# Column maxima of a softmax by VectorE block transposes, and seven VectorE instructions moved, in a fused cross-attention kernel

## The reference

```
proj    = memory @ W_mem.T                       # 1601 x 512
scores  = x @ proj.T / sqrt(512)
attn    = softmax(scores, axis=-1)               # over the 1601 memory rows
ctx     = attn @ proj
gate    = sigmoid(concat(x, ctx) @ W_gate.T + b_gate)
fused   = x + gate * ctx
out     = fused * rsqrt(mean(fused**2) + eps) * norm_w
```

## Time and profile before

| what | us |
|---|---|
| median of 3 runs | 545.79 (545.26 to 546.56) |
| the profiled execution's own time | 546.02 |
| its span | 544.0 |
| PE busy | 533.3 (98% of the span) |
| DVE busy | 480.4 (88%) |
| ACT busy | 315.9 (58%) |
| POOL busy | 148.0 (27%) |
| granted TensorE clock | 0.998 |

### The profile page before, as it was taken

The page is one execution under the profiler, slowest core; times in us unless marked ns, Lnnn a source line. Parts: engine busy times, 40 slices in busy tenths (PEclk is TensorE's granted clock), DMA queues, the critical chain, the costliest instruction groups (busy, mean ns, idle before and its releaser), DMA issues.

```text
span 544.0 us, 8854 instructions
## 1 busy us (share of the span) xinstructions
PE 533.3 (98%) x2420; PEld 436.6 (80%) x2420; DVE 480.4 (88%) x758; ACT 315.9 (58%) x601; POOL 148.0 (27%) x127
## 2 busy tenths in 40 slices
PE   8899999999999999999999999999999999999994
PEld 7776888888888888888888888888888888888883
DVE  3779958899799997999978998989979999789967
ACT  4575636566465664666465763656556575557523
POOL 0005610065002540036200660015400263004703
PEclk9999999999999999999999999999999999999999
DMA  9855363621576207841278214762068510301033
GB/s 225 262 118 92 96 107 88 113 59 41 141 159 104 93 7 170 175 107 39 85 127 171 76 39 125 161 114 72 25 159 169 120 49 30 125 30 40 1 117 116
DMA packets 185861, 56.37 MB, mean 104 GB/s; under 512 B 161756, under 2 KB 175592, under 8 KB 185844
## 3 DMA queue, kind: packets, MB, share of 16 engines
q1 hardware_dynamic: 185316, 55.64, 43.7%
q10 hardware_dynamic: 528, 0.52, 0.3%
HBM read 46.15 MB, written 8.39 MB: 100 GB/s over the span
## 4 chain that ended last, share of the span: by engine, by line
PE 93%; SPq 3%; DMA 2%; DVE 1%; issue 0%; ACTq 0%; POOLq 0%; POOL 0%; DVEq 0%; ACT 0%
PE bank L387 21%; PE bank L389 21%; PE bank L388 21%; PE bank L586 8%; PE bank L587 8%; PE bank L588 8%; DMA fused<-in_L_xattn_W_gate_dram 2%; SPq L262 2%; PE bank L607 1%; PE bank L489 1%; PE bank L621 1%; PE bank L462 1%; PE bank L474 1%; PE bank L570 1%; DMA x_again<-in_x_dram 1%; PE bank L569 1%
## 5 line engine op out<-in xcount | busy, mean ns | idle before, releaser
L1229 POOL TENSOR_TENSOR psum_rows<-psum_rows,p_tmp 128x512 f32<-128x512 f32 (+1 forms) x88 | 122.9, 1397 | 71.6 <-ACT p_tmp L755 70.0
L919 DVE TENSOR_TENSOR p_lo<-p_tmp,p_hi 128x512 fp32r<-128x512 f32 (+1 forms) x104 | 92.6, 891 | 5.5 <-ACT p_hi L716 5.4
L1229 POOL TENSOR_TENSOR psum_rows<-p_tmp 128x512 f32<-128x512 f32 x8 | 10.4, 1297 | 275.2 <-ACT p_tmp L755 275.2
L755 ACT ACTIVATE p_tmp<-s 128x512 f32<-128x512 f32 (+1 forms) x104 | 64.5, 626 | 30.5 <-DVE s L960 29.3
L387 PE MATMUL bank<-q_hi,mt_hi 128*128 128x512 f32 (+1 forms) x208 | 81.9, 394 | 0.0
L389 PE MATMUL bank<-q_hi,mt_lo 128*128 128x512 f32 (+1 forms) x208 | 81.3, 391 | 0.0
L388 PE MATMUL bank<-q_lo,mt_hi 128*128 128x512 f32 (+1 forms) x208 | 81.2, 390 | 0.0
L586 PE MATMUL bank<-p_hi,mem_hi 128*128 128x512 f32 (+1 forms) x196 | 76.4, 390 | 0.0
L587 PE MATMUL bank<-p_lo,mem_hi 128*128 128x512 f32 (+1 forms) x196 | 76.4, 390 | 0.0
L588 PE MATMUL bank<-p_hi,mem_lo 128*128 128x512 f32 (+1 forms) x196 | 76.3, 390 | 0.0
L716 ACT ACTIVATE s<-bank 128x512 f32<-128x512 f32 (+1 forms) x104 | 62.0, 596 | 19.5 <-PE bank L389 19.1
(11 more groups left out here) (98 smaller groups left out, 1031.0 us busy)
## 6 DMA issues: line engine op xcount, KB each, us to landing
mem_raw<-in_ctx_dram SPq DMA_DIRECT2D x48, 256.0 KB, 3.1
mem_blocks<-in_ctx_dram SPq DMA_DIRECT2D x64, 136.0 KB
x_again<-in_x_dram SPq DMA_DIRECT2D x32, 256.0 KB, 2.7
out_dram<-fused SPq DMA_DIRECT2D x32, 256.0 KB, 2.1
x_raw<-in_x_dram SPq DMA_DIRECT2D x112, 64.0 KB, 2.0
mem_blocks<-in_ctx_dram SPq DMA_DIRECT2D x56, 64.0 KB, 2.0
x_raw<-in_x_dram SPq DMA_DIRECT2D x4, 256.0 KB, 5.1
gate<-in_L_xattn_W_gate_dram SPq DMA_DIRECT2D x2, 512.0 KB, 5.6
```

Of the source, the lines that this page charges most:

```text
L755: nc.scalar.activation(p_tmp[0:r, t % TMP_RING, :], s[0:r, t, :], ACT.Exp, scale=float(D) ** -0.5).then_inc(exp_done, 1)
L919: return nc.vector.tensor_tensor(dst, src, hi.bitcast(F32), ALU.subtract)
L1229: nc.gpsimd.tensor_tensor(psum_rows[0:r, :], a, p_tmp[0:r, t % TMP_RING, :], ALU.add).then_inc(p_added, 1)
```

## The change

The column maximum no longer passes TensorE. VectorE transposes `run` in blocks of 32 x 32 into bank 2, reduces each block row to one number (`col_max`, 128 x 16), joins the four groups of 32 partitions by two maxima (64 and 32 partitions), doubles the result twice by copies so that all 128 partitions hold it (`row_max`), and transposes it, each number broadcast 32 times, in blocks into bank 3.

Other VectorE steps move in the iterations behind the first: `mem_lo` 4 and 5 leave the end of the score phase, and 4 goes to softmax tile t = 3, 5 and 6 to t = 10; the bias additions 2 and 3 move from t = 5 and 6 to t = 10; `gate_input` 1, `gate_ctx` 0 and 1 and `add_x` 0 are set between the first three `shift`s in another order; in the loop, outputs 2 and 3 and the next batch's third memory transpose come behind `u_lo`. The text of ScalarE, GpSimd and SyncE is the same.

```
-            def transpose_max(b):
...
-            def spread_max(b, first):
...
+            def column_max(b):
+                dve.wait_ge(s_copied, MT * (b + 1))
+                dve.wait_ge(run_done, (MT - 1) * (b + 1))
+                nc.vector.transpose(blocks(bank[S_BANK][:, :]), blocks(run[:, :])).then_inc(max_blocks, 1)
...
+                nc.vector.tensor_reduce(col_max[:, :], blocks(bank[S_BANK][:, :]), AX.X, ALU.max).then_inc(col_max_done, 1)
...
+                nc.vector.tensor_tensor(pair_max[:, :], col_max[0 : P // 2, :], col_max[P // 2 : P, :],
...
+                nc.vector.tensor_tensor(row_max[0:BLOCK, :], pair_max[0:BLOCK, :], pair_max[BLOCK : 2 * BLOCK, :],
...
+                nc.vector.tensor_copy(row_max[BLOCK : 2 * BLOCK, :], row_max[0:BLOCK, :]).then_inc(max_doubled, 1)
...
+                nc.vector.tensor_copy(row_max[P // 2 : P, :], row_max[0 : P // 2, :]).then_inc(max_copied, 1)
+            def spread_max(b):
+                dve.wait_ge(max_copied, b + 1)
+                nc.vector.transpose(blocks(bank[MAX_BANK][:, :]),
+                                    row_max[:, :].unsqueeze(2).broadcast_to([P, N // BLOCK, BLOCK])).then_inc(max_spread, 1)
...
+        LATE_SPLITS = {3: [4], 10: [5, 6]}
+        BIAS_AT = [3, 4, 10, 10]
...
+                    for q in (SPLIT_BY_SCORES if p < MP - 1 or first else {}).get(p, []):
...
-                    for j in range(NT):
+                    for j in range(NT if last else 2):
                         output(b - 1, j)
...
+                if not last:
+                    transpose_mem(b + 1, 2)
+                    if not first:
+                        output(b - 1, 2)
+                        output(b - 1, 3)
```

More of the change, by code:

```diff
@@ L118, in xattn_kernel @@
         ones = sb("ones", [P, 1])
-        col_max = sb("col_max", [P, NT])
+        col_max = sb("col_max", [P, N // BLOCK])
+        pair_max = sb("pair_max", [P // 2, N // BLOCK])
+        row_max = sb("row_max", [P, N // BLOCK])
         r_sum = sb("r_sum", [P, NT])
@@ L453, in scores @@
                         weights(WG2T[WG2T_AT.index(t)])
-            def transpose_max(b):
-                pe.wait_ge(run_done, (MT - 1) * (b + 1))
-                pe.wait_ge(s_copied, MT * (b + 1))
-                for j in range(NT):
-                    last = nc.tensor.transpose(
-                        bank[S_BANK][:, j * P : (j + 1) * P], run[:, j * P : (j + 1) * P], ident[:, :])
-                last.then_inc(pe_max_t, 1)
-            def spread_max(b, first):
[L469 to L476, removed]
             def row_sums(b, behind_scores):
@@ L1098, in iteration @@
             def iteration(b, first, last):
-                transpose_mem(b, 2)
+                if first:
+                    transpose_mem(b, 2)
                 for p in range(MP):
@@ L1113, in iteration @@
                     dve.wait_ge(in_rows, 32)
-                    reduce_max(b, first)
+                    column_max(b)
+                    spread_max(b)
                     for g in [*WG1T, V[0]]:
@@ L1129, in iteration @@
                 else:
+                    column_max(b)
                     reciprocal(b - 1)
+                    spread_max(b)
                     gate_input(b - 1, 0)
-                    reduce_max(b, first)
+                    gate_input(b - 1, 1)
+                    shift(b, 0)
                     gate_ctx(b - 1, 0)
-                    gate_input(b - 1, 1)
+                    shift(b, 1)
+                    gate_ctx(b - 1, 1)
+                    shift(b, 2)
                     add_x(b - 1, 0)
-                    shift(b, 0)
-                    shift(b, 1)
-                    shift(b, 2)
                     for t in range(MT):
@@ L1142, in iteration @@
                             gate_input(b - 1, t + 1)
-                        if 3 <= t < 3 + NT:
-                            add_bias(b, t - 3, first)
-                        if t in (0, 2, 4):
+                        for j in range(NT):
+                            if t == BIAS_AT[j]:
+                                add_bias(b, j, first)
+                        if t in (2, 4):
                             gate_ctx(b - 1, 1 + t // 2)
@@ L1148, in iteration @@
                             add_x(b - 1, ADD_AT.index(t) + 1)
-                        for q in SPLIT_BY_SOFTMAX.get(t, []):
+                        for q in LATE_SPLITS.get(t, []):
                             mem_lo_part(b, q)
```

27 lines of the change are left out of this document (13 added, 14 removed).

## The result

The changed kernel takes 555.07 us (median of 4 runs, 553.11 to 556.58); the kernel before took 545.63 us beside it (4 runs, 545.26 to 546.56). The ratio is 1.0167, 95% interval 1.0143 to 1.0192: 9.4 us slower. The prediction was 551.0 in a range of 541.5 to 554.5: the direction and the two main causes in the loop were right, the size was not, two places outside the loop were read wrongly, and the time lies 0.6 us outside the range.

What follows compares the result with a forecast made beforehand. TensorE, busy 533.3 of 544.0 us, was taken as the bound. Batch 0 -0.9, iteration 1 +0.3, iterations 2 to 6 +4.6, last batch +1.1 sum to +5.2 on 545.8: 551.0 us, range 541.5 to 554.5.

Steps and rivals of the forecast that it cites:

- the two main causes in the loop: VectorE rows stretched beside GpSimd's additions, 1.2 us more per iteration, and late memory loads, 0.6 us in five iterations.
- the late loads: Batches 2 to 6: later outputs delay SyncE's loads, so ScalarE's tanh and VectorE's gate_ctx 0 come 0.6 us later.
- VectorE's slack at the query: At the next batch's query, the last xt_lo was taken to be ready 2.65 us before TensorE needs it.
- this batch keeps its -0.9: Batch 0: VectorE comes 0.54 us later against 0.72 of slack, so the 0.9 us gain stays, by 0.2.
- everything behind hangs on that TensorE work: Last batch: TensorE waits 2.0 us for u_lo, so the batch ends 1.1 us later.
- what TensorE gives up: Two groups of four transposes leave each batch, 0.44 us each: 0.88 us a batch, 7.0 us over eight.
- what VectorE takes on: Block transposes, reduction, four small steps and the spread transpose add 2.33 us per batch, of which idle time absorbs 0.56.
- Rival 3: VectorE's small steps or broadcast are slower, 0.86 us more in seven batches: 557.5 us; slower than 554 had chance 0.07.
- the contention: VectorE instructions with two SBUF inputs stretch beside GpSimd's additions: 3.7 us up to the last xt_lo, 1.2 more than before.
- 2.33 - 0.56 + 1.2: VectorE's lateness at the last xt_lo: 2.33 us of added work, less 0.56 idle time, plus 1.2 of stretching beside GpSimd.
- The gain stays: Neither surcharge comes and TensorE keeps 0.88 us in seven batches: 539.6 to 540.7 us; chance 0.08.
- One surcharge only: Only GpSimd's stretching comes, 547.8 us, chance 0.14, or only late loads, 543.4, about 545 with half of the stretching.

Runs made afterwards that it cites:

- e12: e11 with the column maxima by TensorE's transposes and batch 0 as in the kernel before: 545.57 us, ratio 1.0003.
- e11: Changed kernel with both add_x moved, memory pair 6 split at tile 11, batch 0's first bias earlier, outputs 2 and 3 ahead of u_lo: 538.68 us.
- e5: Changed kernel with GpSimd's additions of exponentials cut from 512 columns to 8, so outputs are not the reference's: 542.20 us, ratio 0.9927.
- e9: Changed kernel with the second add_x of a batch moved from softmax tile 1 to tile 4: 546.01 us, ratio 1.0002.
- e1: Changed kernel with outputs 2 and 3 in the loop moved up between q_lo and u_lo: 552.97 us, ratio 1.0124.
- e2: Changed kernel with mem_lo 5 and 6 at t = 11 and no longer at t = 10: 555.65 us, ratio 1.0190.
- e4: Changed kernel's column maximum on VectorE, in the instruction order of the kernel before: 554.68 us, ratio 1.0173.
- e7: Changed kernel with the four outputs of batch 6 in the last loop iteration moved behind the two u_lo: 554.16 us, ratio 1.0159.
- e8: Changed kernel with the first bias addition of batch 0 one softmax tile earlier: 556.48 us, ratio 1.0194.
- e13: Changed kernel with eight more, unread matmuls behind the last batch's row sums, where TensorE waits for u_lo: 553.84 us, ratio 1.0160.
- e3: Kernel before, its column maximum still on TensorE, with only the change's moves of VectorE instructions: 554.87 us, ratio 1.0179.

## Why the prediction was off

In the profiles 10.8 us stand where 5.2 were forecast. Three steps of the sum failed. In the loop (2.5 us too little in all) the stalls were the right ones, but the late loads and VectorE's slack at the query were mis-sized. In batch 0 (1.5) the step "this batch keeps its -0.9" failed, and in the last batch (1.7) the step "everything behind hangs on that TensorE work".

**Right: what TensorE gives up.** Forecast 0.88 us a batch, measured 0.95 (e12 against e11). The sum made this too small by 0.5 us in all.

**Right: what VectorE takes on.** The small steps at 0.20, the transposes at 0.72 and 0.73, the reduction at 0.69: all within a few hundredths. Rival 3 (slow steps or a slow broadcast) is out.

**Right, almost to the digit: the contention.** I put +0.79, +0.52, +0.51, +0.23 on `add_x` 1 and `p_lo` 1, 3, 5, and 1.5 us rows for `add_x` 0 and `mem_lo` 4. The rows are 1.46 and 1.50 for the two `add_x` (0.74 unhindered), 1.49 for `mem_lo` 4, and 1.25, 1.18 and 1.00 for the three `p_lo` (0.68): 3.7 us in excess, as forecast. e5 and e9 show that it is what decides: at 2.3 us of excess (e9) the stall at the query is gone. With the maximum's chain it makes the last `xt_lo` start 36.8 us behind the mark in iteration 1, where it was 33.9 before: 2.9 later, forecast 2.33 - 0.56 + 1.2 = 2.97. Instructions with one SBUF input stay clear of it: the `shift` that starts with an addition at 309.19 takes 0.67. This agrees with the Trainium skill, "SBUF — State Buffer", "Who interferes with whom", by which only a VectorE instruction with two SBUF inputs (or in a two-port mode) contends with GpSimd's reads.

**Too small: the late loads.** The chain was right link by link: x loads 7 us late, ScalarE waiting for the DMA ahead of `mem_hi` 4, `tanh` late, `gate_ctx` 0 with 0.96 us of idle time ahead of it. But the forecast was 0.6 us in each of five iterations, and e1 gives 0.84. I had put one part of it (0.3) at the context of piece 2 and the rest at the query. Measured in the iteration from 294.35 on are 0.79 at the context (the product starts at 302.86, the one before at 301.84, and 0.23 is the pitch) and 1.30 at the query (332.99 after 331.46). With TensorE's own 63.16 that is 65.25; the iteration takes 65.66, so some 0.4 is lost in products that come more slowly around the two stalls (product by product beside e11). Of the 2.3 us by which iterations 2 to 6 are worse than forecast, the loads are 1.2 (five times 0.24).

**Too large: VectorE's slack at the query.** The other 1.1 is a stall that is 0.3 us an iteration longer than my sum (1.5 in five iterations, less the 0.35 that TensorE gave up beyond the forecast). Iteration 1 and all of e1 have it too, without late loads: 64.65 - 63.16 = 1.49 where I had 1.2. VectorE was not later than forecast; the slack of 2.65 that I set against it was too large. I took it from the end of the `xt_lo` row to the start of the query. But where TensorE waits, the query starts 0.14 us behind that end (332.99 for 332.85), so the slack was 2.51; and its products start more slowly behind a wait (332.99, then 333.32 instead of 0.23 later), so that from the query to the next mark it takes 27.0 us, where e11 takes 26.9. By these figures the stall is 2.91 - (2.51 - 0.94) + 0.13 = 1.47.

**Wrong: batch 0.** "This batch keeps its -0.9, by a margin of 0.2" was made at the query alone. The first batch has only two banks for its `gate_x` pieces, so the third piece needs the bank that bias 0 frees. That wait was not near the query, and I checked only the wait that bounds the loop. TensorE loses

```profile
52.63 0.50 PE L393 MATMUL bank<-wg1t_hi,xt_hi 128*128 128x512 f32 x1 [1.34 <-DVE gate L988]
```

there. 0.88 gained, 1.34 lost: +0.5, and the table has +0.6. That these agree so well is partly luck, since the arrival of the weights moves the first mark by more. Where TensorE is busy for all of the stretch from 20 to 30 us, the mark is at 96.96 with the old batch 0 (e12) and at 97.68 to 97.78 with the changed one (e2, e4, e7): +0.7 to +0.8.

**Wrong: the last batch.** The wait came as forecast: the first product of `u` starts 43.31 us behind the sums of batch 6, where it was 42.26 before, +1.05 for a forecast of +1.1. What failed is the step "everything behind hangs on that TensorE work": it assumed the work behind at its old pace. The nine products at the lowered clock take 1.7 us more than before, and 1.05 + 1.7 is the 2.8 that was measured. The kernel before never shows a granted clock under 1.00 while TensorE works, so no row priced this; but the list of what a wait costs should have had a line for it, and the upper end of the range with it.

**Rivals.** The gain stays (539.6 to 540.7): no, although e11 shows that this is what the change gives once VectorE has room. One surcharge only: the changed kernel has both. e1 and e5 take away one each, and only e5, without the contention, comes down below the kernel before.

What stays open: loop iterations 2 to 6 of the changed kernel spread over 0.5 us where e1's agree within 0.04. The spread is that of the late `tanh`: the waits of TensorE for `gate_ctx`, 0.27, 0.23, 0.64, 0.74 and 0.40 us, are in the same order of size as the iterations, 65.32, 65.27, 65.66, 65.77 and 65.41. Which load is late in which iteration I haven't followed. Not tried: GpSimd's additions themselves at other places, or on another engine. No run takes the late loads and the contention out of the changed kernel and leaves the rest as it is; e11 takes out both, but moves other instructions too.

## What to carry to other kernels

Before work is moved onto an engine that isn't the bound, count its slack at every place where the bound engine meets it, the first and the last batch included, measured up to the moment at which a waiting engine would have started and not to the end of the row, and count it again with the instructions that GpSimd stretches: they cost nothing as long as the slack covers them, and their full length from the moment it doesn't. If the sum ends at zero, as this one did, look for the cheapest microsecond first: here moving one two-SBUF-input instruction into a pause of GpSimd was worth 9 us over the kernel, and only with that in place did the change show its 0.95 us a batch. Halves of a change that draw on one slack don't add up: each alone cost as much as both.

## What the runs showed of the hardware

A TensorE that had run at a granted clock of 1.00 paused, 2.0 us from the start of one matmul to that of the next, and then had nine to fourteen matmuls some 0.43 us apart instead of 0.23, at 0.50 (1.2 GHz) (the changed kernel, e1, e8; in e2 six came at the full pace first, and then about eight slow ones); with eight matmuls put into the gap it stayed at 1.00 (e13). After shorter gaps the rows go both ways: 1.5 us between starts at the same place in e3 was followed by seven slow products, 1.1 us in e4 and the 1.5 us ahead of the query by none. VectorE's block transpose of 128 x 512 from SBUF to PSUM took 0.73 us and the same with a broadcast input 0.72, so reading one column 32 times cost nothing. And the start of the kernel differs by about 1.5 us from one execution to the next with the arrival of the weights (TensorE busy for 8.61 or 10.00 us of the stretch from 20 to 30; in the kernel before it waits 1.39 us there for a load of the gate's weights, in e12 not at all), which is as much as some of the steps that I meant to weigh there.
